# Decoder layer with routed experts: experts' rows weighted on the way out of PSUM and added to the tokens' rows in DRAM by accumulating indirect DMAs

## What is computed

```python
logits = einsum('bsd,ed->bse', x2, gate_w)
scores = softmax(logits).transpose(0, 2, 1)           # (b, e, s)
topk_w, topk_idx = top_k(scores, 32)                  # each expert takes 32 tokens of each sequence
x_tok = x2[b, topk_idx]                               # (b, e, 32, 256)
h = gelu(x_tok @ Wg[e].T) * (x_tok @ Wu[e].T)         # 512 hidden
eo = (h @ Wd[e].T) * topk_w[..., None]
out[b, topk_idx] += eo                                # scatter-add over all experts
shared = (gelu(x2 @ Ws_g.T) * (x2 @ Ws_u.T)) @ Ws_d.T
y = layernorm(x2 + out + shared)
```

## Time and profile before

| | |
|---|---|
| median of 3 runs | 3314.11 us (3310.68 to 3316.03) |
| the profiled execution | 3313.88 us |
| its span (first to last instruction) | 3312.2 us |
| mean granted TensorE clock | 0.98 of full speed |
| TensorE busy | 96% of the span |
| DVE, ACT, POOL busy | 71%, 66%, 41% |
| experts' stage | about 2371 to 2950 us |
| `combine` | about 2950 us to the end |

### The profile page before, as it was taken

The page is one execution under the profiler, slowest core; times in us unless marked ns, Lnnn a source line. Parts: engine busy times, 40 slices in busy tenths (PEclk is TensorE's granted clock), DMA queues, the critical chain, the costliest instruction groups (busy, mean ns, idle before and its releaser), DMA issues. The chain is left out here.

```text
span 3312.2 us, 80850 instructions
## 1 busy us (share of the span) xinstructions
PE 3182.4 (96%) x23456; PEld 2995.9 (90%) x23456; DVE 2348.6 (71%) x6770; ACT 2198.0 (66%) x7067; POOL 1359.3 (41%) x2767
## 2 busy tenths in 40 slices
PE   5999999999999968999999999999699999989999
PEld 4999999999999958999999999999588888879999
DVE  5777777777777756777778778787454544537777
ACT  5888788888878756777777777777344444424433
POOL 3666666667666643333333333333422222200000
PEclk8999999999999989999999999999799999999999
DMA  5444444444444430001010101001233333324443
GB/s 176 109 116 127 125 120 122 122 117 116 128 126 119 115 97 15 26 26 30 27 33 24 33 24 36 24 27 40 74 96 114 101 101 111 98 70 121 120 120 102
DMA packets 201355, 283.79 MB, mean 86 GB/s; under 512 B 33344, under 2 KB 149952, under 8 KB 200384
## 3 DMA queue, kind: packets, MB, share of 16 engines
q1 hardware_dynamic: 194880, 262.91, 27.7%
q0 software_dynamic: 6144, 16.79, 1.7%
HBM read 124.41 MB, written 41.94 MB: 50 GB/s over the span
## 5 line engine op out<-in xcount | busy, mean ns | idle before, releaser
L863 POOL TENSOR_SCALAR ca_prob<-ca_prob,ca_inverse 128x120 f32<-128x120 f32 x1024 | 355.0, 366 | 650.5 <-DVE ca_inverse L1179 648.5
L603 ACT ACTIVATE sa_prob<-sa_prob,sa_shift 128x128 f32<-128x128 f32 (+1 forms) x1024 | 453.4, 460 | 7.4 <-DVE sa_shift L644 6.0
L1107 ACT ACTIVATE ca_prob<-bank,ca_shift 128x120 f32<-128x120 f32 x1024 | 355.9, 370 | 5.1 <-DVE ca_shift L1173 4.3
L644 DVE CUSTOM_DVE_ANT_0 sa_prob<-bank,sa_mask 128x128 f32<-128x128 f32 (+1 forms) x1024 | 304.4, 352 | 9.1 <-issue 4.8
L411 POOL TENSOR_SCALAR sa_prob<-sa_prob,sa_inverse 128x128 f32<-128x128 f32 x512 | 197.2, 385 | 244.0 <-DVE sa_inverse L652 234.4
L1401 POOL DMA_INDIRECT first_x_raw<-mid_x,ex_tokens x124 | 131.2, 1058 | 381.1 <-PE bank L1438 349.4
L131 PE MATMUL bank<-sa_ow,sa_y_hi 128*128 128x256 f32 x1024 | 278.0, 303 | 0.0
L131 PE MATMUL bank<-sa_kvT_a,sa_q 128*128 128x128 f32 (+1 forms) x1024 | 253.5, 284 | 21.7 <-DMA sa_q<-sa_q_tile 12.1
L133 PE MATMUL bank<-sa_kvT_b,sa_q 112*128 112x128 f32 (+1 forms) x1024 | 261.2, 280 | 0.0
L675 DVE TENSOR_TENSOR sa_pT_lo<-bank,sa_pT_hi 128x384 fp32r<-128x384 f32 x512 | 258.1, 543 | 0.6 <-ACT sa_pT_hi L590 0.6
L133 PE MATMUL bank<-sa_ow,sa_y_lo 112*128 112x256 f32 x1024 | 256.8, 282 | 0.0
(11 more groups left out here) (265 smaller groups left out, 12378.9 us busy)
## 6 DMA issues: line engine op xcount, KB each, us to landing
sa_q<-sa_q_tile SPq DMA_DIRECT2D x128, 288.0 KB
sa_q<-sa_q_tile SPq DMA_DIRECT2D x160, 112.0 KB
mid_eo<-ex_out SPq DMA_DIRECT2D x32, 512.0 KB, 3.0
co_eo_raw<-mid_eo SPq DMA_DIRECT2D x128, 128.0 KB, 2.7
sa_q<-sa_q_tile SPq DMA_DIRECT2D x304, 32.0 KB
sa_xT_raw<-in_xT SPq DMA_DIRECT2D x32, 256.0 KB, 3.0
sa_q<-sa_q_tile SPq DMA_DIRECT2D x32, 256.0 KB
sa_x_res<-in_x SPq DMA_DIRECT2D x32, 256.0 KB, 2.9
```

Source lines behind the costliest of these rows:

```text
L603: act.activation(prob[:, r, hh, cols], prob[:, r, hh, cols], ACT.Exp, bias=shift[:, r, n:n + 1], scale=-1.0, accum_out=total[:, r, n:n + 1 ...
L644: dve.tensor_tensor_reduce(out=prob[:, r, hh, cols], in0=SC[hh][:, t * T:t * T + (t + 1) * P], in1=mask[:].rearrange("p a s -> p (a s)")[: ...
L863: ins = pool.tensor_scalar(prob[:, r, t, hh], prob[:, r, t, hh], inverse[:, r, n:n + 1], 1.0, ALU.mult, ALU.mult)
L1107: act.activation(prob[:, r, t, hh], SC[g % 2][:, n * S:n * S + S], ACT.Exp, bias=shift[:, r, n:n + 1], accum_out=total[:, r, n:n + 1]).the ...
```

## The change

A second copy of `x2` in DRAM, `acc`, is written by cross attention beside `x2`. The experts' rows are multiplied by their weights as ACT and DVE copy them out of PSUM, now 256 columns (128 rows' outputs) at a time, since the weight is one number per partition and tile. POOL then adds each 128 rows of `out` to the tokens' rows in `acc` with an indirect DMA that accumulates; there are four for a chunk, 128 in all. A chunk's accumulates wait for those of the chunk before to have landed. In POOL's stream they come after the gathers of a chunk four further on. `combine` reads `x_res` from `acc` in place of `x2`, and the placing products and all that prepared them are gone, and so are `eo`, its stores and its loads. `weight_col` and `index_col` become one `weight_of`, laid out like `token_of`.

```diff
 # cross_attention, SP
-                        sp.dma_start(d["x2"][J * SEQS + (i - 3)].rearrange("(t p) c -> p t c", p=P), x2[:, k]).then_inc(x2_out[k], 16)
+                        for to in ("x2", "acc"):
+                            sp.dma_start(d[to][J * SEQS + (i - 3)].rearrange("(t p) c -> p t c", p=P), x2[:, k]).then_inc(x2_out[k], 16)
...
 # cross_attention, ACT
-                        for q in range(Q4):
-                            ins = act.activation(weight_col[q * CAP:(q + 1) * CAP, bass.ds((J + u) * SEQS, SEQS)].rearrange("c b k o -> c b (k o)"),
-                                                 VALUE_T.rearrange("c (b k q) -> c q b k", k=KS, q=Q4)[:, q], ACT.Copy)
+                        for q in range(SEQS):
+                            ins = act.activation(weight_of[q * CAP:(q + 1) * CAP, :, bass.ds(J + u, 1)].rearrange("c e o -> c (e o)"),
+                                                 VALUE_T[:, q * E:q * E + E], ACT.Copy)
...
 # cross_attention, DVE
-                        for q in range(Q4):
-                            ins = dve.tensor_copy(index_col[...], INDEX_T...)
...
 # experts, SP
-                    m = n - DL - 1
-                    if exists(J, m):
-                        need(sp, act_out, n_of(J, m))
-                        need(sp, dve_out, n_of(J, m))
-                        rows = d["eo"][J * 2 + m // CHUNKS].rearrange("b c f -> (b c) f")
-                        sp.dma_start(rows[...].rearrange("(t p) f -> p t f", p=P), out[:, m % 2]).then_inc(stored[m % 2], 16)
...
 # experts, POOL (behind the gathers of chunk n)
+                    m = n - XBODY
+                    if exists(J, m):
+                        if n % CHUNKS == 0:
+                            for k in range(2):
+                                need_alone(pool, added[k], added_by(J, m - 2 + k), spare_pool)
+                            pool.tensor_copy(to_tokens[:, e], token_of[:, J * 2 + (e - 2)]).then_inc(to_tokens_done, 1)
+                            need_alone(pool, to_tokens_done, J * 2 + (e - 1), spare_pool)
+                        need_alone(pool, added[1 - i], added_by(J, m - 1), spare_pool)
+                        need_alone(pool, act_out, n_of(J, m), spare_pool)
+                        need_alone(pool, dve_out, n_of(J, m), spare_pool)
                         for t in range(TILES):
                             j = (n % CHUNKS) * TILES + t
+                            pool.indirect_dma_start(d["acc"].rearrange("b t c -> (b t) c"),
+                                                    bass.IndirectOffsetOnAxis(ap=to_tokens[:, e, j:j + 1], axis=0), out[:, i, t], None,
+                                                    compute_op=ALU.add).then_inc(added[i], 16)
...
+            for i in range(2):
+                pool.wait_ge(added[i], 16 * TILES * E * CHUNKS // 2)
...
 # experts, ACT
-                        need(act, d_mm, n_of(J, n, 2, -1))
-                        need(act, stored[i], (J * (8 * XBODY) + 16 * (n // 2)))
-                        act.activation(out[:, i, 0:2].rearrange("p t f -> p (t f)"), DB[0][:], ACT.Copy).then_inc(act_out, 1)
+                        need(act, added[i], added_by(J, n - 2))
+                        need_alone(act, d_mm, n_of(J, n, 2, -1), spare_act)
+                        for t in range(2):
+                            j = (n % CHUNKS) * TILES + t
+                            ins = act.activation(out[:, i, t], DB[0][:, t * C:t * C + C], ACT.Copy,
+                                                 scale=weight_of[:, J * 2 + n // CHUNKS, j:j + 1])
+                        ins.then_inc(act_out, 1)
...
 # experts, DVE: the same for its half
-                        dve.tensor_copy(out[:, i, 2:4].rearrange("p t f -> p (t f)"), DB[1][:]).then_inc(dve_out, 1)
+                        for t in range(2, TILES):
+                            j = (n % CHUNKS) * TILES + t
+                            ins = dve.tensor_scalar(out[:, i, t], DB[1][:, (t - 2) * C:(t - 1) * C], weight_of[:, J * 2 + n // CHUNKS, j:j + 1],
+                                                    None, ALU.mult)
+                        ins.then_inc(dve_out, 1)
...
 # combine, SP
-                        need(sp, eolo_done, upto_two(J, i - 2, KS))
-                        for q in range(P // CAP):
-                            sp.dma_start(eo_raw[q * CAP:(q + 1) * CAP, i],
-                                         d["eo"].rearrange("(k q) b c f -> q b c k f", k=KS)[q, J * 2 + i]).then_inc(eo_in[i], 16)
...
-                        sp.dma_start(x_res[:], d["x2"][J * 2 + (i - 2)].rearrange("(t p) c -> p t c", p=P)).then_inc(res_in, 16)
+                        sp.dma_start(x_res[:], d["acc"][J * 2 + (i - 2)].rearrange("(t p) c -> p t c", p=P)).then_inc(res_in, 16)
...
 # combine, PE
-                        need(pe, hot_done, upto_two(J, b))
-                        need(pe, eolo_done, upto_two(J, b, KS))
...
-                            for k in range(KS):
-                                pe.matmul(to, onehot[:, i, k, ts], eo_hi[:, i, k], start=False, stop=False, skip_group_check=True)
-                                mm = pe.matmul(to, onehot[:, i, k, ts], eo_lo[:, i, k], start=False, stop=k == KS - 1,
-                                               skip_group_check=True)
...
 # combine, ACT
-                        need(act, eo_in[i], J * 64 + 64 * (b // 2 + 1))
-                        need_alone(act, d_mm, upto_two(J, b - 2), spare_act)
-                        for k in range(KS):
-                            act.activation(eo_hi[:, i, k], eo_raw[:, i, k], ACT.Copy,
-                                           scale=weight_col[:, J * 2 + b, k]).then_inc(eohi_done, 1)
+                        need(act, d_mm, upto_two(J, b - 2))
...
 # combine, DVE
-                        for k in range(KS):
-                            ins = dve.tensor_scalar(onehot[:, i, k], token_row[:], index_col[:, J * 2 + b, k], None, ALU.is_equal)
-                        ins.then_inc(hot_done, 1)
...
-                        for k in range(KS):
-                            need(dve, eohi_done, upto_two(J, b, KS, k - KS + 1))
-                            dve.scalar_tensor_tensor(out=eo_lo[:, i, k], in0=eo_raw[:, i, k], scalar=weight_col[:, J * 2 + b, k],
-                                                     in1=f32(eo_hi[:, i, k]), op0=ALU.mult, op1=ALU.subtract).then_inc(eolo_done, 1)
```

More of the change, by code:

```diff
@@ L703, in _, with cross_attention @@
             over_bodies(dve, body, 2, SA_BODIES - 1, SA_BODIES + 1)
-def cross_attention(nc, bank, ident, index_col, weight_col, token_of, first, wv_raw, wv_in, d):
+def cross_attention(nc, bank, ident, weight_of, token_of, first, wv_raw, wv_in, d):
     with ExitStack() as ctx:
@@ L1326, in load_expert, with experts @@
                      d[name][e].rearrange("(k p) n -> p k n", p=P)).then_inc(loaded, 16)
-def experts(nc, bank, ident, token_of, ahead, first, d):
+def experts(nc, bank, ident, weight_of, token_of, ahead, first, d):
     with ExitStack() as ctx:
@@ L1557, in combine @@
         xT_hi, xT_lo = al.split("xT", [P, 2, KC, T])
-        eo_raw = al.sb("eo_raw", [P, 2, KS, C])
-        eo_hi, eo_lo = al.split("eo", [P, 2, KS, C])
-        onehot = al.sb("onehot", [P, 2, KS, T], F32R)
         act_g = al.sb("act_g", [P, 2, 2, T])
@@ L1571, in combine @@
         x_in = [al.sem(f"x_in{i}") for i in range(2)]
-        eo_in = [al.sem(f"eo_in{i}") for i in range(2)]
         y_out = [al.sem(f"y_out{i}") for i in range(2)]
@@ L1760, in program @@
         token_of = al.sb("token_of", [P, E, GATHERS], U32)
[L1761 to L1762 removed]
+        weight_of = al.sb("weight_of", [P, E, GATHERS])
         made = al.sem("made")
@@ L1776, in program @@
             self_attention(nc, bank, ident, wv_raw, wv_in, d)
-            cross_attention(nc, bank, ident, index_col, weight_col, token_of, first, wv_raw, wv_in, d)
+            cross_attention(nc, bank, ident, weight_of, token_of, first, wv_raw, wv_in, d)
         with ExitStack() as moe:
             ahead = ExpertWeights(Alloc(nc, moe, "ahead"), first)
-            experts(nc, bank, ident, token_of, ahead, first, d)
-            combine(nc, bank, ident, index_col, weight_col, ahead.shared, d)
+            experts(nc, bank, ident, weight_of, token_of, ahead, first, d)
+            combine(nc, bank, ident, ahead.shared, d)
 def kernel(**inputs):
```

63 lines of the change are left out of this document (26 added, 37 removed).

## The result

The kernel after takes 3272.45 us (median of 4 runs, 3269.76 to 3273.01) against 3312.76 (4 runs, 3310.68 to 3316.03): a ratio of 0.9876, 95% interval 0.9859 to 0.9893. It is faster by 40 us, not by the 54.7 of the sum, and lies 1.5 us above the range.

A forecast was written before the change was run, and what follows sets the result against it. TensorE was taken to bound the experts' stage and `combine`. Terms -60.8 + 7.3 + 0.1 - 1.5 - 0.7 + 0.9 made -54.7 us, from 3313.9 to a forecast 3259 us, range 3253 to 3271.

The forecast's parts named there:

- The experts' tail: End of the experts' stage: the last two chunks' accumulates lie in the open, +7.3 us, bounds +4.3 and +10.3.
- Placing products: Last stage: two runs of eight matmuls per sequence go, 1.90 us each sequence, -60.8 us over 32, step 8.89 us.
- The head of `combine`: Start of the last stage: the second sequence loads earlier, so its transposes start sooner, -1.5 us, bounds 0 and -2.5.
- fourth accumulate starts 4.09 later: End of the experts' stage: four accumulates take 4.09 us from first start to last, as four gathers do.
- if its issue too costs twice: End of the experts' stage: should an accumulate's issue cost twice a gather's, the two rounds of issuing add 8.2 us.
- L: Time for an accumulate to land, in the experts' tail: taken as 4.3 us, between bounds of 2.8 and 5.8.
- then 0.95: End of the experts' stage: about 0.95 us from the last landing to the next stage's first load.
- The rule on adding DMAs: Skill's claim that adding DMAs run at half a copy's rate; by it alone landing about 5.6 us, tail +9.9.
- Steady state of the accumulates: Experts' stage: POOL has 10.1 us of work in a 17.6 us chunk, so accumulates there cost nothing.
- The first rival: Experts' stage: accumulates bind POOL, slower than before; at 4.2 us each 130 us more, some 3390; chance 0.05.
- The experts' stage still 17.6 us per chunk: Sign that the forecast is right: the experts' stage keeps its time per chunk, unchanged at 17.6 us.
- Cross attention: End of that stage: DVE's four `index_col` copies ahead of the barrier go, -0.7 us; the extra store costs nothing.

The follow-up runs named there:

- e3_plain_scatter: The kernel after with plain indirect writes in place of the accumulating ones, so rows are overwritten and not added to: 3268.4 us, ratio 0.9865.
- e1_place_gone: The kernel before with only the last stage's placing products, their preparation and the loads of `eo` taken out: 3252.57 us, ratio 0.9816.
- e10_cross_only: The kernel before without the placing products and with the cross attention of the kernel after, experts' code and addresses as before: 3253.03 us, ratio 0.981.
- e4_layout: The kernel after with its tiles put back at the addresses they have in the kernel before, nothing else changed: 3269.0 us, ratio 0.9868.
- e5_sp_waits: The kernel after with the wait for the last additions' landing moved from GpSimd to SyncE: 3271.85 us, ratio 0.988.
- e9_plain_copies: The kernel after with tiles at the addresses of before and unweighted 512-column copies out of PSUM as before: 3265.88 us, ratio 0.9847.
- e6_pair: The kernel after without the wait between the two chunks of one expert for the first one's additions to land: 3269.53 us, ratio 0.9876.

## Why the prediction was wrong, point by point

Two steps failed. The experts' tail was sized with a gather's issue and a store's end of stage: +7.3 us, and it measured +13.8. And the experts' stage was taken to keep its 17.6 us a chunk because the change leaves its matmuls alone; it takes 17.84, since a new tile moved their operands.

- **Placing products, -60.8.** Right: step 8.88 (predicted 8.89), last stage -61.2 with head and end; alone -60.7. VectorE's 1.2 us of slack were enough. The head of `combine` too: the second transposes start 2.62 us after the first (2970.45, 2973.07), and the end of the program loses what was said.
- **The experts' tail, +7.3: the term was too small, the measured one is +13.8.** The mechanism was right (two rounds of four, the second waiting for the first to land), and its size failed in three steps. From the end of the last copy but one (2942.53) to SyncE's load (2967.70) it takes 25.2 us where the working has 17.8. First, the step "fourth accumulate starts 4.09 later" took a gather's issue: it is 5.57 and 5.55, together +2.9. Its own bound, "if its issue too costs twice", was the one to take. Second, from the fourth start to the next round it took 4.72 where L was 4.3, +0.4: the landing came after 3.8 us, inside the bounds, but the working had no time from a landing to the next issue. And the first issue came 0.8 after the copy, +0.7. Third, "then 0.95" for the end of the block: from the fourth issue it is 8.54 and not L + 0.95 = 5.25, +3.3. That 0.95 was read from a stage end in which GpSimd had long been idle. (Of these 7.3 some 0.8 don't reach the gap, mainly because the last copy ends 0.3 later behind the one before it, and the first load takes 2.75 to the transposes and not 3.05.)
- **The rule on adding DMAs.** The Trainium skill (Collectives: The Full Stack, "The bandwidth ceiling: the fold count and why AG ≠ RS ≠ AR") names two source reads, and half the rate, for the adding step of a ring collective. The packets agree in direction (three where a plain one makes one). The half rate doesn't show in the landing, which comes after 3.8 us and not after 5.6, a gather's being 2.8. Of this 1.0 us, 0.6 is the issue, 1.57 us against 0.97.
- **Steady state of the accumulates, nothing.** Right: without them the chunk is no shorter (17.91). GpSimd is busy for 357.92 of 573.40 us there, 11.1 a chunk. Every second chunk one accumulate takes some 3.8 us (14 of the 128 take 3.59 to 3.85), and each of these stands beside one of VectorE's 3.36 us splits of weights:

```profile
2891.82 3.84 POOL L1406 DMA_INDIRECT mid_acc<-ex_out,ex_to_tokens  x1 [0.30 <-issue]
...
2890.87 3.36 DVE L1522 TENSOR_TENSOR ahead_w_lo<-ahead_w_raw,ahead_w_hi 128x3072 fp32r<-128x3072 f32 x1 [1.80 <-ACT ahead_w_hi L1475]
```

  All 14 end 1.43 to 1.45 us after the split does. In `e3_plain_scatter` 14 plain scatters stand beside a split, and all of them end 0.86 us after it. Both are 0.1 us short of a whole issue (1.57 and 0.97), as if nearly all of the issue had to wait for the split's end, and it doesn't come with adding. The first rival needed 3.6 us for all four, not for one in nine. The Trainium skill (DMA: Bandwidth & Descriptors, "SWDGE vs HWDGE vs iDMA") has VectorE in its two-port modes lock GpSimd out while it writes descriptors. I gave that little weight by the median; the long ones look like a lockout by VectorE, though they cost nothing here. Whether the split, a `tensor_tensor`, runs in such a mode, no run here shows.
- **"The experts' stage still 17.6 us per chunk": wrong, +9.0.** This is the larger part of the miss beside the tail, and no step of the prediction looked at it: it takes for granted that untouched matmuls keep their pace. 64 bytes ahead of the tiles made the kernel before 8.3 us longer. Of the 9.0 some 1.4 are the clock's, as said above.
- **Cross attention, -0.7: too small.** From first transposes to last `token_of` or `index_col` it takes 1134.8 us after against 1139.4, and 3.6 us of gain over `e1_place_gone` are seen in `e10_cross_only`. Beside `index_col` an idle time of VectorE's at the end is gone (2.44 us at 2364.98 before, for which the trace names no wait; the other two kernels with the old code have it too) and a shorter one has come (0.77 us). The rest of the -5.8 is self attention, whose code is the same in all kernels and whose end varies by 4.8 us over the thirteen profiles (cross attention begins between 1225.1 and 1229.9). That part is luck.
- **Outside the span, +2.4, not foreseen.** Some 4.1 us there in the kernel after, `e3_plain_scatter`, `e4_layout`, `e5_sp_waits` and `e9_plain_copies`; 1.7 to 1.8 in all others. `e6_pair` differs from the kernel after by one wait in GpSimd's loop, and has 1.7. Its cause is open.

The misses add up: +6.5 in the gap, +8.9 in the experts' stage, -5.1 ahead of them, +0.2 in `combine` and +2.4 outside the span are +12.9, from -54.7 to -41.8. Without the 5.1 us ahead of the experts, a part of them luck, the time would lie further above the range. The range counted the tail's unknowns, but no unknown for the stage that the change left alone.

## What to carry to other kernels

Price an accumulating indirect DMA by its own row, not by a gather's, and where a stage ends with GpSimd's DMAs, count its way out of the stage: moved into the next stage, they cost nothing. Adding a small tile ahead of TensorE's operands made a whole stage 1.5% longer here; compare start-to-start distances of matmuls that the change didn't touch, and put the addresses back before judging the change. Where code that is the same in two kernels differs in pace, look for the event that is released late before blaming the edit.

## What the runs showed of the hardware

- TensorE's pace follows the addresses of its tiles in SBUF: 0.1154 us for 256 columns at the old ones (0.1196 in 3 to 8 chunks of 30 there) and 0.1203 with 64 bytes put ahead of them; 0.229 or 0.233 against 0.232 for 512. All at full granted clock and without waits.
- An accumulating indirect DMA of 128 rows of 1 KB: 1.57 us of issue against 0.97 plain, landing 3.8 us after the issue starts against a gather's 2.8, three packets for one.
- An indirect DMA that GpSimd issues beside VectorE's 3.36 us `tensor_tensor` of weights is held up until that one is over: the accumulates end 1.43 to 1.45 us after it, the plain scatters 0.86.
- GpSimd leaves a stage slowly after its own DMAs: SyncE's next load comes some 5 us after the last byte if GpSimd waited for it, 2.4 us if SyncE did, and 0.8 us after the last copy where GpSimd's last DMA was well before.
- The gap of 20.85 us cost little more of the low clock than one of 7.03: matmuls of 256 columns start 0.21 us apart for 4.1 us from 2974.16 in the kernel after, for 3.0 us from 2958.64 before, and 0.12 apart from then on (granted clock 0.5 until 2978.14 and 2961.48, 1.0 behind that). That is some five matmuls more at 0.09 us, 0.5 us.
